# Expert weight halves stored as one transfer per piece, with the down matrix in column blocks of 128

## What is computed

```python
x = x + xattn0(layernorm(x), ctx, seg_id, ...)    # 16 heads, 128 keys a row
x = x + moe(layernorm(x), gate_w, w_gate, w_up, w_down)
x = x + xattn1(layernorm(x), ctx, mask)
x = x + ffn1(layernorm(x), ...)                    # gated MLP and 8 of 1024 retrieved experts

# moe(): E = 16, MOE_D = 352, K = 6
scores = softmax(h @ gate_w.T); topk_w, topk_idx = top_k(scores, 6)
for e in range(E):
    out = (silu(h @ w_gate[e].T) * (h @ w_up[e].T)) @ w_down[e].T
    y = y + cw[:, e:e + 1] * out
```

## Time and profile of the kernel before

| what | us |
|---|---|
| median of 3 executions | 1945.56 |
| lowest and highest of them | 1942.91, 1946.44 |
| the profiled execution, device time | 1929.01 |
| its span in the trace | 1927.2 |
| PE busy in the span | 1803.6 |
| first attention, with the splitting of the weights | about 106 to 575 |
| from there to the first expert block | about 575 to 617 |
| experts | 617 to 1320 |
| second attention and last feed forward | 1320 to 1927 |

### The profile page before, as it was taken

The page is one execution under the profiler, slowest core; times in us unless marked ns, Lnnn a source line. Parts: engine busy times, 40 slices in busy tenths (PEclk is TensorE's granted clock), DMA queues, the critical chain, the costliest instruction groups (busy, mean ns, idle before and its releaser), DMA issues.

```text
span 1927.2 us, 39654 instructions
## 1 busy us (share of the span) xinstructions
PE 1803.6 (94%) x12786; PEld 1075.3 (56%) x12789; DVE 1096.7 (57%) x2985; ACT 886.3 (46%) x1833; POOL 819.4 (43%) x731
## 2 busy tenths in 40 slices
PE   6989999999982999999999999995899999999998
PEld 3566667666641666666666666664644444444444
DVE  4678887888862333322323223223756877777776
ACT  4578878878851443434434434443832121122211
POOL 4224456666564334444443443442112434554442
PEclk8999999999986999999999999997999999999999
DMA  8255598878886566666666665545012355555653
GB/s 309 88 153 175 177 140 182 188 166 175 184 183 181 143 147 141 155 165 149 153 155 142 155 152 100 90 85 129 33 35 72 124 182 201 205 170 209 208 174 144
DMA packets 156354, 294.83 MB, mean 153 GB/s; under 512 B 41248, under 2 KB 91040, under 8 KB 152032
## 3 DMA queue, kind: packets, MB, share of 16 engines
q1 hardware_dynamic: 105184, 157.48, 30.4%
q0 software_dynamic: 46368, 126.29, 26.8%
q10 hardware_dynamic: 4608, 8.52, 1.6%
HBM read 426.00 MB, written 78.33 MB: 262 GB/s over the span
## 4 chain that ended last, share of the span: by engine, by line
PE 63%; DMA 15%; DVE 9%; issue 6%; ACT 5%; SPq 1%; POOL 1%; POOLq 0%; ACTq 0%; DVEq 0%
PE bank L235 16%; PE bank L236 16%; PE bank L237 16%; DMA x_sum<-x,work_arena 10%; DVE work_arena L1580 2%; PE bank L1064 2%; ACT xt_arena L1316 2%; DMA work_arena<-in_moe_w 2%; PE bank L854 1%; PE bank L1091 1%; DVE xt_arena L1580 1%; PE bank L1175 1%; DMA expert_w<-xt_arena 1%; DMA x<-token_rows,work_arena 1%; DVE xt_arena L1663 1%
## 5 line engine op out<-in xcount | busy, mean ns | idle before, releaser
L235 PE MATMUL bank<-work_arena,xt_arena 128*128 x1221 | 404.6, 331 | 2.8 <-DVE xt_arena L2074 1.9
L237 PE MATMUL bank<-work_arena,xt_arena 128*128 x1221 | 404.5, 331 | 0.0
L236 PE MATMUL bank<-work_arena,xt_arena 128*128 x1221 | 404.5, 331 | 0.0
L2313 POOL DMA_INDIRECT x_sum<-x,work_arena x111 | 175.9, 1585 | 397.7 <-DMA x_sum<-x,work_arena 197.2
L2062 DVE TENSOR_TENSOR xt_arena<-xt_arena,bank 128x352 f32<-128x352 f32 x111 | 57.9, 522 | 406.2 <-PE bank L237 406.2
L235 PE MATMUL bank<-work_arena 128*128 128x512 f16 (+1 forms) x600 | 226.8, 379 | 13.9 <-DVE x L1885 6.7
L236 PE MATMUL bank<-work_arena 128*128 128x512 f16 (+1 forms) x600 | 226.7, 379 | 0.0
L237 PE MATMUL bank<-work_arena 128*128 128x512 f16 (+1 forms) x600 | 226.6, 379 | 0.0
L1470 ACT ACTIVATE xt_arena<-bank 128x1024 f16<-128x1024 f16 x111 | 113.6, 1023 | 224.8 <-PE bank L1064 224.8
L235 PE MATMUL bank<-xt_arena,work_arena 128*128 128x512 f16 x528 | 200.4, 380 | 1.8 <-DVE xt_arena L195 1.8
L236 PE MATMUL bank<-xt_arena,work_arena 128*128 128x512 f16 x528 | 200.3, 379 | 0.0
(11 more groups left out here) (278 smaller groups left out, 3817.5 us busy)
## 6 DMA issues: line engine op xcount, KB each, us to landing
work_arena<-expert_w SPq DMA_DIRECT2D x111, 1408.0 KB
work_arena<-expert_w SPq DMA_DIRECT2D x111, 768.0 KB
work_arena<-in_moe_w SPq DMA_DIRECT2D x64, 352.0 KB
expert_w<-work_arena SPq DMA_DIRECT2D x128, 176.0 KB
work_arena<-in_moe_w SPq DMA_DIRECT2D x64, 192.0 KB
expert_w<-xt_arena SPq DMA_DIRECT2D x128, 96.0 KB
work_arena<-in_mlp_w SPq DMA_DIRECT2D x8, 1536.0 KB, 9.0
work_arena<-in_head_w SPq DMA_DIRECT2D x16, 512.0 KB, 5.2
```

What stands on the lines that cost most here:

```text
L235: pe.matmul(o, a_hi, b_hi, start=start, stop=False)
L236: pe.matmul(o, a_hi, b_lo, start=False, stop=False)
L237: return pe.matmul(o, a_lo, b_hi, start=False, stop=stop)
L2313: pool.indirect_dma_start(out=xacc[:, :], out_offset=bass.IndirectOffsetOnAxis(ap=rid[:, i:i + 1], axis=0), in_=ysb[:, b % YB, :], in_offs ...
```

## The change

The two halves of a piece get one staging tile of twice the width, high half first, and one DMA stores both. Each of these stores has 128 rows of 2816 bytes (gate and up) or 1536 bytes (down) in place of twice 1408 or twice 768. The device memory row of an expert now holds hi and lo of each piece side by side. For the gate and up part a piece is one chunk of input rows, so the slices that `expert_up` reads stay 352 neighbouring columns, only at other offsets. A down piece is now 128 output columns of all three chunks of hidden rows, so the moving operand of a down matmul is four runs of 128 fp16 values (256 bytes), 1536 bytes apart; the host lays `moe_w` out to fit. The output in PSUM is the same 512 neighbouring columns. The staging tiles lie at the same addresses as before, since both halves were taken one behind the other then too.

```diff
 PIECES = [piece for c in range(4) for piece in (
-    (c * UP_N, UP_N, c * UP_N, AW + c * UP_N),
-    (AW + c * DOWN_N, DOWN_N, 2 * AW + c * DOWN_N, 2 * AW + DW + c * DOWN_N))]
+    (c * UP_N, UP_N, 2 * c * UP_N), (AW + c * DOWN_N, DOWN_N, 2 * AW + 2 * c * DOWN_N))]
...
-            sp_hi[s] = room.take(n, dt=F16)
-            sp_lo[s] = room.take(n, dt=F16)
+            sp16[s] = room.take(2 * n, dt=F16)
...
             def split_store(i):
-                e, (_, n, hi_at, lo_at), s = i // NPC, PIECES[i % NPC], i % STAGES
+                e, (_, n, at), s = i // NPC, PIECES[i % NPC], i % STAGES
                 sp.wait_ge(split_lo, i + 1)
-                for t, at in ((sp_hi, hi_at), (sp_lo, lo_at)):
-                    sp.dma_start(wsp[e, :, at:at + n], t[s][:, 0:n]).then_inc(split_out[s], 16)
+                sp.dma_start(wsp[e, :, at:at + 2 * n], sp16[s][:, 0:2 * n]).then_inc(split_out[s], 16)
...
-                        hi, lo = (wa[:, ds(base + (k * AW + (2 * d + i) * MOE_D), MOE_D)] for k in range(2))
+                        hi, lo = (wa[:, ds(base + (4 * d + 2 * k + i) * MOE_D, MOE_D)] for k in range(2))
...
+                w = wd[:, ds(base, 2 * DW)].rearrange("p (q k c n) -> p q k c n", q=4, k=2, c=3)
                 for c in range(3):
-                    hi, lo = (wd[:, ds(base + (k * DW + c * D), D)] for k in range(2))
-                    m = mm3(pe, bank[6 + b % 2][:, :], ehT[:, b % 2, c * P:(c + 1) * P],
+                    hi, lo = w[:, :, 0, c, :], w[:, :, 1, c, :]
+                    m = mm3(pe, bank[6 + b % 2][:, :].rearrange("p (q n) -> p q n", q=4), ehT[:, b % 2, c * P:(c + 1) * P],
...
-                    need(act, split_out[s], i // STAGES * 32)
-                    act.activation(sp_hi[s][:, 0:n], sp32[s][:, 0:n], ACT.Copy, scale=WS).then_inc(split_hi, 1)
+                    need(act, split_out[s], i // STAGES * 16)
+                    act.activation(sp16[s][:, 0:n], sp32[s][:, 0:n], ACT.Copy, scale=WS).then_inc(split_hi, 1)
...
-                    lo_of(sp_lo[s][:, 0:n], sp32[s][:, 0:n], WS, sp_hi[s][:, 0:n]).then_inc(split_lo, 1)
+                    lo_of(sp16[s][:, n:2 * n], sp32[s][:, 0:n], WS, sp16[s][:, 0:n]).then_inc(split_lo, 1)
...
-    dn = dn.reshape(E, 3, P, D).transpose(0, 2, 1, 3).reshape(E, P, DW)
+    dn = dn.reshape(E, 3, P, 4, P).transpose(0, 2, 3, 1, 4).reshape(E, P, DW)
```

More of the change, by code:

```diff
@@ L447, in build @@
         pw_room.at = pw_at
-        sp32, sp_hi, sp_lo = {}, {}, {}
+        sp32, sp16 = {}, {}
         for s in (0, 2):
@@ L660, in split_load @@
             def split_load(i):
-                e, (at, n, _, _), s = i // NPC, PIECES[i % NPC], i % STAGES
+                e, (at, n, _), s = i // NPC, PIECES[i % NPC], i % STAGES
                 if i >= STAGES:
@@ L686, in _ @@
             for s in range(STAGES):
-                sp.wait_ge(split_out[s], 32 * len(range(s, E * NPC, STAGES)))
+                sp.wait_ge(split_out[s], 16 * len(range(s, E * NPC, STAGES)))
             sp.wait_ge(yadd, 1)
```

## The result

The changed kernel takes 1930.66 us (median of 5 runs, 1926.74 to 1934.56), beside it the kernel before 1945.56 (5 runs, 1940.36 to 1951.59): ratio 0.9919, 95% interval 0.9897 to 0.994. But the two profiled executions differ by almost nothing: span 1925.0 after, 1927.2 before. What follows grows out of that contradiction.

What follows compares the result with a forecast made beforehand. It took PE as the bound, full in the expert stage, with few idle microseconds in the attention for DMA relief to reach. Terms -1.0 - 1.8 - 3.0 + 0 = -5.8 us, from 1945.6 to 1939.8; range 1934 to 1949.

Steps and rivals of the forecast that it cites:

- The base: Whole kernel: run median 16.6 us above the profiled execution, taken as shared by both kernels, so 1945.6 - 5.8 = 1939.8.
- Faster: Whole kernel: the outcome that the change makes it faster, chance 0.46, beside same 0.39 and slower 0.15.
- The packets: Piece stores in the attention: 16384 fewer packets, worth 18 to 55 us of 16 engines, DMA shares down 5 to 15 points.
- my lower end of 18: DMA engines: 18 ns for a packet beside its bytes, from two lightly loaded stretches; the loaded stretch gave up to 54.
- a price of 3.5 ns: DMA engines: fixed packet cost estimated from the Trainium skill, relief some 4 us; the rows were said to disagree fivefold.
- (a) near 400: Attention: a load 1 to 2 us earlier removes most of PE's 1.3 us wait behind ACT; 1.0 us gained, bounds 0 and 1.3.
- (b) the end of the attention: Last two loads land earlier, so PE's 1.83 us wait for DVE's add goes; 1.8 us gained, bounds 0 and 4.
- The tail: Between attention and experts: first expert load 3.5 us earlier, row store and last list entry land earlier; 3.0 us, bounds 0 and 3.8.
- floor of 4.91: Last list entry before the experts: at least 4.91 us, an expert-stage indirect DMA's time, so 601.6 against 605.44, at most 3.8 us.
- the relief stays hidden: Rival, attention: packets are cheap or DVE and POOL set the idle times; 1945, 0 to -2 us, chance 0.27.
- The down matmuls: Expert stage: 999 matmuls with a moving operand of four 256-byte runs cost 0 extra; upper bounds 6 to 8 or 69 us.
- More relief than counted: Rival: clock holds at the attention's end and small DVE and ACT waits shrink throughout; -12 us, 1934, chance 0.03.

Runs made afterwards that it cites:

- e_oneissue2: One DMA stores both halves of a piece, with the old layout, packet sizes and down operand, against the kernel before on chip 13: ratio 0.9914 (0.9887 to 0.9942).

## Why the prediction was wrong

**The base** is where it failed. The text says of the 16.6 us between the profiled execution and the median that "both kernels should share that". They don't: the changed kernel's profiled execution (1926.74) is one of its timed ones, 3.9 us below their median. The chips fall into two kinds for this kernel: before takes 1917 to 1928 on chips 0, 6 and 10 and 1946 to 1947 on chips 2 and 13. The profile before, at 1929.0, holds a single one of PE's unexplained stops (1.0 us, ahead of all list writes) and none of ACT's waits, as on chips of the first kind; by their times the timed runs were of the second, and so was the changed kernel's profile by its waits on ACT. The 16.6 us were, nearly, the thing that the change removes: PE's stops, 23.8 us in before and 8.9 in the changed kernel on chip 13. No row that I had could show it. The gap itself was the sign: the three timed runs lie within 3.5 us of one another and the profiled one 14 us below the lowest, and I explained that by nothing. "Faster" came true by this mechanism, which the prediction doesn't have; its own terms gave nothing that can be seen, so the direction was luck.

**The packets.** The count was right: SP's queue has 18432 packets fewer (105184 to 86752), and the shares fell by 3, 4 and 8 points of the 5 to 15 forecast. From 160 to 560 the queue's share fell from 70.6% to 67.0% for 15942 packets. Put down to the packets alone that is 0.036 x 16 x 400 us / 15942 = 14 ns each, under my lower end of 18. But the packets aren't what lowers it. The queue from 160 to 560 in the kernel with one DMA and the old packets, then in the changed kernel, first on chip 10, then on chip 13:

```profile
q1 hardware_dynamic: 45866, 61.10, 66.3%
q1 hardware_dynamic: 31618, 61.20, 67.3%
```
```profile
q1 hardware_dynamic: 45981, 61.26, 67.8%
q1 hardware_dynamic: 31513, 61.04, 66.4%
```

14248 packets fewer go with a share 1.0 point higher on chip 10, and 14468 fewer with one 1.4 points lower on chip 13, which would be 6 ns a packet. Most of the fall comes with the second transfer (before has 69.1% on chip 10). So the cost of a packet, with which the prediction's relief begins, was set too high by a factor of three at least, and its finding that the rows exclude a price of 3.5 ns doesn't hold. The lower share bought nothing that can be seen on chip 10, and `e_oneissue2` has nearly the packets of before and gains.

**(a) near 400**, 1.0 us: right in this pair of profiles. ACT's 3.58 us for a piece are gone and with them PE's 1.3 us for ACT; all of PE's waits from 380 to 420 fall from 2.6 to 1.3 us. But before on chip 10 has no such wait of PE there either, so it comes and goes between executions.

**(b) the end of the attention**, 1.8 us: right in part. The loads come in time, and everything stands 4.2 us earlier (557.90 for the matmul that started at 562.12). But PE's wait for DVE's add is 2.79 us, not gone, so the text was wrong that "the 1.83 us go". The 3.26 us for POOL ahead of it are what stayed, as said (4.03 before).

**The tail**, 3.0 us: the first half held, with the load 4.4 us earlier for 3.5 forecast. The second failed. "Both the row store and the last entry land earlier" is wrong: SP's list load is at 606.14, not 602, since the last entry took 11.17 us, 2.5 more than before, and the row store, too, landed later, at 605.7 for 604.7. Its floor of 4.91, taken from another kind of transfer in the expert stage, didn't bind. The first expert matmul is at 613.58, and was at 614.36: 0.8 us won by all local terms together, of 5.8. Even that mixes two kinds of chip; on chip 10 the changed kernel's is 0.9 us later than that of before (613.23 and 612.29). On chip 10, then, the rival "the relief stays hidden" describes what happened: nearly nothing.

**The down matmuls**, 0: right. 0.22 us apart in the trace, and ratios 1.0002 and 0.9995 for layout and operand alone. The interval of the latter, up to 1.0019, bounds a jump between runs at 3.7 us / 2997, 1.2 ns. The Trainium skill (Advanced Engine Details and Errata, "Memory Cachelines") says of PSUM that any non-contiguous access slows a matmul down; the output here stays contiguous, so the runs don't try that sentence. Its sentences on SBUF ask only that accesses in a row hit the same 16 bytes, and the runs agree with them for this moving operand in SBUF.

**The rivals.** "More relief than counted" gave 1934 and was built on small waits that shrink; the size came out near by luck, with another mechanism.

**What is shown and what isn't.** Shown: the gain is there on chips 2 and 13 and not on chip 10, it comes from one transfer less for each piece, and most of it lies in stops of PE in front of matmuls that wait for nothing. Seen in every profile of chips 2 and 13, but not tested: the stops stand behind the sixth list write of a tile. No kernel moved or dropped those writes; that is the run to make next. Why PE stops there, why ACT waits behind the third write and whether the two are one thing is open. An idea of mine, that PE's instructions come late over the busy DMA engines, agrees badly with the trace: on chip 13 PE stopped before its matmuls at 433.45 and 434.86 for 1.92 and 1.20 us, and no queue carried an instruction block from 423.5 to 433.5. What distinguishes the two kinds of chip is open too, and so is whether the number of transfers or their order counts.

## What to carry to other kernels

When the profiled execution and the timed runs of the same kernel differ by more than the effect that you forecast, that difference is a stage of the kernel that your trace doesn't show: get a trace of a run that has it before you sum. Where SP issues transfers in pairs for one piece of work beside indirect DMAs of POOL, joining them into one DMA can be worth more than its packets, even if its rows stay as they were (12 to 20 us on two chips here, nothing on a third). Don't take a packet's price from stretches that differ in more than packets; change only the packets and compare on one chip. Don't join further than the slots allow: a store that waits for a second piece holds the first one's buffer, and that costs more than any transfer saved.

## What the runs showed of the hardware

- The same kernel takes 1917 to 1928 us on three chips and 1946 to 1947 on two others, each met once. The difference lies in the stretch with many transfers and not in the expert stage, where PE at the full granted clock is equally fast on both.
- On the slower two PE stops for up to 2.7 us at a time, and 4.6 us in one tile, inside matmuls without waits, repeatedly at the same place of the program, often by lengths near 1.20 and 1.92 us. With its idle time the granted clock goes down as well: 0.97 in before and 1.00 in the changed kernel from 300 to 450 on chip 13.
- On the same two ACT starts a copy 1.9 to 3.0 us after the transposes that it waits for have ended, in 9 or 10 tiles of every kernel, behind the third of POOL's indirect DMAs of the tile. On the other three it never does.
- A matmul of 512 columns whose moving operand is four runs of 256 bytes costs what one of 512 neighbouring columns does, to within 3.7 ns.
- 14000 packets fewer at the same bytes and the same number of DMAs moved the share of SP's queue by +1.0 point on one chip and -1.4 on another: at most some 6 ns a packet.
